# A decoder's linear attention on one Trainium2 core: one reciprocal, keys by a maximum, sums in one pass

## The reference, cut to what matters

```python
for i in range(8):
    residual = x
    Q  = elu(x @ Wq[i] + bq[i]) + 1
    Kf = elu(x @ Wk[i] + bk[i]) + 1
    V  = x @ Wv[i] + bv[i]
    KV, sumK = sum over positions of Kf * V, of Kf
    Z  = 1 / (Q * sumK + 1e-6)
    att = Q * KV * Z
    x = layer_norm(gelu(att @ Wo[i] + bo[i]) + residual)
    residual = x
    x = layer_norm(gelu(gelu(x @ W1[i] + b1[i]) @ W2[i] + b2[i]) + residual)
```

## Time and profile before

| what | value |
|---|---|
| median of three runs | 3417.19 us (3416.45 to 3419.0) |
| span of the profiled execution | 3428.6 us |
| PE, DVE busy | 88%, 79% of the span |
| ACT, POOL busy | 56%, 39% |

### The profile page before, as it was taken

The page is one execution under the profiler, slowest core; times in us unless marked ns, Lnnn a source line. Parts: engine busy times, 40 slices in busy tenths (PEclk is TensorE's granted clock), DMA queues, the critical chain, the costliest instruction groups (busy, mean ns, idle before and its releaser), DMA issues. The chain is left out here.

```text
span 3428.6 us, 44182 instructions
## 1 busy us (share of the span) xinstructions
PE 3029.2 (88%) x11560; PEld 2029.0 (59%) x11561; DVE 2711.6 (79%) x8902; ACT 1927.6 (56%) x2995; POOL 1323.7 (39%) x1039
## 2 busy tenths in 40 slices
PE   5698989898989898999899989998999976998995
PEld 4465656565656565666566655665566644776553
DVE  8879888988898889888988898889888834763111
ACT  4566666666666666666666666666666622442221
POOL 5325343534353435343534353435443323333002
PEclk9899999999999999999999999999999987997998
DMA  4001100100011001000100010001000001003312
GB/s 102 17 1 24 25 16 18 24 25 16 18 24 25 16 18 24 25 16 18 24 25 16 18 24 25 16 18 24 18 24 4 1 0 49 0 0 131 100 40 74
DMA packets 212286, 93.22 MB, mean 27 GB/s; under 512 B 146792, under 2 KB 207984, under 8 KB 212048
## 3 DMA queue, kind: packets, MB, share of 16 engines
q1 hardware_dynamic: 209408, 83.30, 9.6%
q0 software_dynamic: 2640, 7.21, 0.6%
HBM read 80.24 MB, written 10.22 MB: 26 GB/s over the span
## 5 line engine op out<-in xcount | busy, mean ns | idle before, releaser
L350 PE MATMUL PS<-XTHI,WHI 128*128 128x512 f32 x1536 | 672.6, 438 | 38.1 <-DVE EK L654 27.9
L285 POOL TENSOR_TENSOR INV<-INV,CE 128x512 f32<-128x512 f32 x256 | 305.9, 1195 | 984.1 <-DVE INV L697 984.1
L646 DVE SCALAR_TENSOR_TENSOR RK<-RK,EK 128x128 f32<-128x128 f32 x1024 | 599.6, 638 | 28.7 <-ACT RK L515 0.5
L351 PE MATMUL PS<-XTLO,WHI 128*128 128x512 f32 x1536 | 610.7, 398 | 0.0
L352 PE MATMUL PS<-XTHI,WLO 128*128 128x512 f32 x1536 | 609.9, 397 | 0.0
L398 PE MATMUL Y<-ATT,WO 128*128 128x512 f32 x1024 | 468.5, 612 | 59.8 <-POOL ATT L289 59.4
L398 PE MATMUL Y<-H,W2S 128*128 128x512 f32 x1024 | 465.9, 609 | 51.9 <-DVE R L708 50.4
L289 POOL TENSOR_TENSOR ATT<-INV,CC 128x512 f32<-128x512 f32 x256 | 316.7, 1237 | 195.5 <-PE Y L398 177.9
L398 PEld LDWEIGHTS Y<-ATT,WO 128*128 128x128 f32 x1024 | 197.7, 196 | 301.0 <-issue 298.2
L350 PEld LDWEIGHTS PS<-XTHI,WHI 128*128 128x128 f32 x1536 | 291.4, 190 | 133.2 <-issue 42.3
L398 PEld LDWEIGHTS Y<-H,W2S 128*128 128x128 f32 x1024 | 197.0, 195 | 290.4 <-issue 227.2
(11 more groups left out here) (195 smaller groups left out, 5440.7 us busy)
## 6 DMA issues: line engine op xcount, KB each, us to landing
STAGE<-L_attn_Wk SPq DMA_DIRECT2D x128, 64.0 KB, 2.1
STAGE<-L_attn_Wv SPq DMA_DIRECT2D x128, 64.0 KB, 2.1
STAGE<-L_attn_Wq SPq DMA_DIRECT2D x128, 64.0 KB, 2.1
WO<-L_attn_Wo SPq DMA_DIRECT2D x8, 1024.0 KB, 5.5
W2S<-L_attn_W SPq DMA_DIRECT2D x8, 1024.0 KB, 6.1
STAGE<-L_attn_W SPq DMA_DIRECT2D x64, 128.0 KB, 3.7
RAW<-L_ffn_r_gate SPq DMA_DIRECT2D x8, 512.0 KB, 3.5
RAW<-L_ffn_r_up SPq DMA_DIRECT2D x8, 512.0 KB, 3.6
```

The lines of the kernel that those rows point to most:

```text
L285: nc.gpsimd.tensor_tensor(r3, r3, spread(CE[:, e, :], SEQ), ALU.mult).then_inc(att_s, 1)
L350: nc.tensor.matmul(out, whi[:, kc, :], xhi[:, kc, :], start=(kc == 0), stop=False)
L351: nc.tensor.matmul(out, whi[:, kc, :], xlo[:, kc, :], start=False, stop=False)
L646: ins = nc.vector.scalar_tensor_tensor(RK[:, p, seq(b)], RK[:, p, seq(b)], 0.0, EK[:, p, seq(b)], ALU.add, ALU.add, accum_out=SUMK[:, p, b ...
```

## The change

In the attention stack alone:

- ACT no longer computes `RK`, nor log and exp of the denominator. Its table set for the attention is the one with exp alone. A small `BUP` = key bias + 1 is made twice a layer.
- Keys: `KK[.., 0, ..]` = the larger of (PSUM + `BUP`) and the rounded exp, one DVE instruction over 512; `KK[.., 1, ..]` = that times V, one instruction over 512; then one reduction over both (1024 elements to 8 sums, `SUMS`).
- Four operations on 128x4 (`factors`) in place of five; they move from the end of `keys` to the start of `queries`.
- One DVE reciprocal of 128x512, in place in `EQ`, directly behind the denominator, in place of log, exp, `residues` and `inverses`. `attend` reads `EQ`.
- PE waits for `kf` (DVE) where it waited for `rk` (ACT), and for `kv_mul` where it waited for `kv_sum`. ACT waits for `att` where it waited for `recip` before it overwrites `EQ`.

```diff
+        BUP = sb("BUP", [P, HC])
...
-        EK = sb("EK", [P, 2, TOK])
-        RK = sb("RK", [P, 2, TOK])
+        KK = sb("KK", [P, 2, 2, TOK])
...
-        INV = sb("INV", [P, IRING, TOK])
...
-        SUMK = sb("SUMK", [P, 2, TS])
-        KVS = sb("KVS", [P, 2, TS])
-        RSK = sb("RSK", [P, 2, TS])
+        SUMS = sb("SUMS", [P, 2, 2, TS])
...
@@ -280,8 +276,8 @@
                 g, e = l * TILES + t, c % IRING
                 n = g * HC + c
                 pool.wait_ge(recip, n + 1)
-                pool.wait_ge(stat, n * 5 + 5)
-                r3 = INV[:, e, :].rearrange("p (b s) -> p b s", b=TS)
+                pool.wait_ge(stat, n * 4 + 4)
+                r3 = EQ[:, e, :].rearrange("p (b s) -> p b s", b=TS)
                 nc.gpsimd.tensor_tensor(r3, r3, spread(CE[:, e, :], SEQ), ALU.mult).then_inc(att_s, 1)
                 pool.wait_ge(att_s, n + 1)
...
 
-                return [(rk, n - 1), (kv_sum, n - 1), (rq, n - 1)]
+                return [(kf, n - 1), (kv_mul, n - 1), (rq, n - 1)]
...
                     if m < 3:
-                        pe.wait_ge((rk, kv_sum, rq)[m], chunks)
+                        pe.wait_ge((kf, kv_mul, rq)[m], chunks)
...
                 if t == 0 and c % 4 == 0:
                     cs = slice(c, c + 4)
                     act.wait_ge(ba_in[c // 4], (l + 1) * 48)
+                    nc.scalar.add(BUP[:, cs], BA[:, 0, cs], 1.0)
                     nc.scalar.mul(BNEG[:, :, cs], BA[:, :, cs], -1.0).then_inc(b_neg, 1)
                     act.wait_ge(b_neg, 2 * l + (c // 4 + 1))
                 act.wait_ge(k_mm, n + 1)
                 if not (type(n) is int and n < 2):
                     act.wait_ge(kv_sum, n - 1)
-                nc.scalar.activation(EK[:, p, :], PS[:, half, :], ACT.Relu, scale=-1.0,
+                nc.scalar.activation(KK[:, p, 0, :], PS[:, half, :], ACT.Relu, scale=-1.0,
                                      bias=BNEG[:, 0, c:c + 1]).then_inc(nk, 1)
-                nc.scalar.activation(RK[:, p, :], PS[:, half, :], ACT.Relu, bias=BA[:, 0, c:c + 1]).then_inc(rk, 1)
                 act.wait_ge(nk, n + 1)
-                nc.scalar.activation(EK[:, p, :], EK[:, p, :], ACT.Exp, scale=-1.0).then_inc(ek, 1)
+                nc.scalar.activation(KK[:, p, 0, :], KK[:, p, 0, :], ACT.Exp, scale=-1.0).then_inc(ek, 1)
                 act.wait_ge(q_mm, n + 1)
                 if not (type(n) is int and n < IRING):
-                    act.wait_ge(recip, n - (IRING - 1))
+                    act.wait_ge(att, n - (IRING - 1))
                 nc.scalar.activation(EQ[:, c % IRING, :], PS[:, half + 2, :], ACT.Relu, scale=-1.0,
...
 
-            def invert(l, t, c):
-
-                n, e = (l * TILES + t) * HC + c, c % IRING
-                act.wait_ge(denom, n + 1)
-                if not (type(n) is int and n < IRING):
-                    act.wait_ge(att, n - (IRING - 1))
-                nc.scalar.activation(INV[:, e, :], EQ[:, e, :], ACT.Ln).then_inc(log, 1)
-                act.wait_ge(log, n + 1)
-                nc.scalar.activation(INV[:, e, :], INV[:, e, :], ACT.Exp, scale=-1.0).then_inc(inv, 1)
-
             def attention_tables():
 
-                nc.scalar.preload_act_table_set("natural_log_exp_and_others")
+                nc.scalar.preload_act_table_set("exp_and_others")
...
                 if exists(l, t + 2):
-                    invert(nl, nt, 7)
+                    attention_tables()
                     al, at = slot_of(l, t + 2)
                     chunk(al, at, 0)
...
                 n = (l * TILES + t) * HC + c
                 p, e, half = c % 2, c % IRING, 3 * (c % 2)
                 dve.wait_ge(ek, n + 1)
-                nc.vector.tensor_scalar(EK[:, p, :], EK[:, p, :], -1.0, 1.0, ALU.add, ALU.add).then_inc(k_exp, 1)
-                dve.wait_ge(rk, n + 1)
+                nc.vector.tensor_scalar(KK[:, p, 0, :], KK[:, p, 0, :], -1.0, 1.0, ALU.add, ALU.add).then_inc(k_exp, 1)
+                if t == 0 and c % 4 == 0:
+                    dve.wait_ge(b_neg, 2 * l + (c // 4 + 1))
                 dve.wait_ge(k_exp, n + 1)
-                for b in range(TS):
-                    ins = nc.vector.scalar_tensor_tensor(RK[:, p, seq(b)], RK[:, p, seq(b)], 0.0, EK[:, p, seq(b)],
-                                                         ALU.add, ALU.add, accum_out=SUMK[:, p, b:b + 1])
-                ins.then_inc(k_sum, 1)
+                nc.vector.scalar_tensor_tensor(KK[:, p, 0, :], PS[:, half, :], BUP[:, c:c + 1], KK[:, p, 0, :],
+                                               ALU.add, ALU.max).then_inc(kf, 1)
                 dve.wait_ge(v_mm, n + 1)
-                if t == 0 and c % 4 == 0:
-                    dve.wait_ge(ba_in[c // 4], (l + 1) * 48)
-                dve.wait_ge(k_sum, n + 1)
-                for b in range(TS):
-                    ins = nc.vector.scalar_tensor_tensor(EK[:, p, seq(b)], PS[:, half + 1, seq(b)], BA[:, 1, c:c + 1],
-                                                         RK[:, p, seq(b)], ALU.add, ALU.mult,
-                                                         accum_out=KVS[:, p, b:b + 1])
-                ins.then_inc(kv_sum, 1)
-                nc.vector.tensor_scalar(SUMK[:, p, :], SUMK[:, p, :], TINY, None, ALU.max).then_inc(stat, 1)
-                dve.wait_ge(stat, n * 5 + 1)
-                nc.vector.reciprocal(RSK[:, p, :], SUMK[:, p, :]).then_inc(stat, 1)
-                dve.wait_ge(stat, n * 5 + 2)
-                nc.vector.tensor_scalar(ES[:, p, :], RSK[:, p, :], EPS_ATT, None, ALU.mult).then_inc(stat, 1)
+                dve.wait_ge(kf, n + 1)
+                nc.vector.scalar_tensor_tensor(KK[:, p, 1, :], PS[:, half + 1, :], BA[:, 1, c:c + 1], KK[:, p, 0, :],
+                                               ALU.add, ALU.mult).then_inc(kv_mul, 1)
+                dve.wait_ge(kv_mul, n + 1)
+                nc.vector.tensor_reduce(SUMS[:, p, :, :], KK[:, p, :, :].rearrange("p k (b s) -> p k b s", b=TS),
+                                        AX.X, ALU.add).then_inc(kv_sum, 1)
+
+            def factors(l, t, c):
+
+                n = (l * TILES + t) * HC + c
+                p, e = c % 2, c % IRING
                 dve.wait_ge(kv_sum, n + 1)
+                nc.vector.tensor_scalar(SUMS[:, p, 0, :], SUMS[:, p, 0, :], TINY, 1.0 / EPS_ATT, ALU.max,
+                                        ALU.mult).then_inc(stat, 1)
+                dve.wait_ge(stat, n * 4 + 1)
+                nc.vector.reciprocal(ES[:, p, :], SUMS[:, p, 0, :]).then_inc(stat, 1)
+                dve.wait_ge(stat, n * 4 + 2)
                 if not (type(n) is int and n < IRING):
                     dve.wait_ge(att, n - (IRING - 1))
-                nc.vector.tensor_tensor(CC[:, e, :], KVS[:, p, :], RSK[:, p, :], ALU.mult).then_inc(stat, 1)
-                dve.wait_ge(stat, n * 5 + 4)
-                nc.vector.tensor_tensor(CE[:, e, :], CC[:, e, :], ES[:, p, :], ALU.mult).then_inc(stat, 1)
-
-            def queries(l, t, c, before=True):
-
+                nc.vector.scalar_tensor_tensor(CC[:, e, :], SUMS[:, p, 1, :], 1.0 / EPS_ATT, ES[:, p, :], ALU.mult,
+                                               ALU.mult).then_inc(stat, 1)
+                dve.wait_ge(stat, n * 4 + 3)
+                nc.vector.scalar_tensor_tensor(CE[:, e, :], CC[:, e, :], -1.0, ES[:, p, :], ALU.mult,
+                                               ALU.mult).then_inc(stat, 1)
+
+            def queries(l, t, c):
 
                 n = (l * TILES + t) * HC + c
                 p, e = c % 2, c % IRING
+                factors(l, t, c)
                 dve.wait_ge(eq, n + 1)
                 nc.vector.tensor_scalar(EQ[:, e, :], EQ[:, e, :], -1.0, 1.0, ALU.add, ALU.add).then_inc(q_exp, 1)
-                if before and not (type(n) is int and n < 1):
-                    residues(n - 1, (c - 1) % HC)
                 dve.wait_ge(rq, n + 1)
                 dve.wait_ge(q_exp, n + 1)
-                dve.wait_ge(stat, n * 5 + 3)
                 for b in range(TS):
                     ins = nc.vector.scalar_tensor_tensor(EQ[:, e, seq(b)], EQ[:, e, seq(b)], ES[:, p, b:b + 1],
                                                          RQ[:, p, seq(b)], ALU.add, ALU.add)
                 ins.then_inc(denom, 1)
-                if before and not (type(n) is int and n < 1):
-                    inverses(n - 1, (c - 1) % HC)
-
...
+                dve.wait_ge(denom, n + 1)
+                nc.vector.reciprocal(EQ[:, e, :], EQ[:, e, :]).then_inc(recip, 1)
...
-                    queries(nl, nt, 7, False)
+                    queries(nl, nt, 7)
                 if exists(l, t + 2):
                     al, at = slot_of(l, t + 2)
-                    n = (g + 2) * HC
-                    residues(n - 2, HC - 2)
-                    inverses(n - 2, HC - 2)
-                    residues(n - 1, HC - 1)
-                    inverses(n - 1, HC - 1)
```

(38 more changed lines are left out.)

## The result

The changed kernel takes 3817.9 us (median of four runs, 3813.8 to 3820.6) against 3418.1 us before: 11.6% slower, ratio 1.1164 with a 95% interval of 1.1148 to 1.118. The forecast was 3643 us, so the sign was right and the size about half of what came (226 us said, 400 measured).

What follows compares the result with a forecast made beforehand. PE and DVE were taken as near-equal bounds, DVE setting the end after the change. Reciprocal +791, holding -399 and filled waits -166 gave +226 us: span 3655, median 3643 us, 6.6% slower; range 3480 to 3820.

Steps and rivals of the forecast that it cites:

- DVE becomes the bound, one for one: Attention stack: work added to DVE beyond 5.2 us a slot lengthens the slot one for one; PE waits longer.
- The reciprocal's price: DVE's 128x512 reciprocal in each chunk: 5.9 ns an element, 3.17 us, giving +791 us of DVE time.
- the three prices that I weighed: Reciprocal's cost an element above the floor, from small reciprocals: 4.5, 5.9 or 7.25 ns; 5.9, from the longer row, taken.
- The unheld chunk: DVE's chunk with nothing in the way: 6.05 us before, and again 6.05 us after, leaving the whole reciprocal over.
- The waits filled: DVE's waits for exp and inverse fill up: -166 us, as DVE would lag behind ACT and PE instead.
- The holding: DVE held by POOL on the sums (L646) and Newton steps: all of it goes, -399 us.
- holding comes back elsewhere: Rival: POOL holds roundings, small operations and denominators for half of what is saved, +200, 3843 us; chance 0.08.
- the signs that I had named: Right: reciprocal near 3.2 us, exp waits almost gone, more PE waiting. Wrong: reciprocal under 2.3 us, denominators' mean far above 350 ns.
- a steeper reciprocal: Rival: DVE's reciprocal costs 7.25 ns an element, 179 us more, 3822 us; chance 0.17.
- two other rivals: Holding comes back elsewhere (3843 us, chance 0.08); DVE's waits don't fill, up to +166, 3809 us, chance 0.08.

Runs made afterwards that it cites:

- Half the reciprocal: The changed kernel with the reciprocal over the first 256 of its 512 columns, the other half left uninverted: 3464.3 us, ratio 1.0115.
- the passes moved ahead: The changed kernel with GpSimd's two attend passes of chunks 2 and 5 issued ahead of the norms' rstd: 3722.5 us, ratio 1.0857.
- ATT elsewhere: The changed kernel with the two passes to ATT done by ScalarE (four activations a chunk), none by GpSimd: 3621.1 us, ratio 1.0555.
- the keys' part alone: The kernel before with only the change's keys' maximum, product, reduction and four small operations; log, exp and Newton steps stay: 3268.1 us, ratio 0.9541.
- the reciprocal alone: The kernel before with only the reciprocal replacing log, exp, residues and inverses; keys computed as before: 3775.4 us, ratio 1.103.

## Why the prediction was right in its sign and half in its size

- *DVE becomes the bound, one for one.* Right. DVE's waits for inputs were 166 us and are 1.4. Half the reciprocal, the passes moved ahead, and ATT elsewhere each moved the time by what they took from DVE, less the waits that came back: 354 for 410 - 56, 95 for 97, 197 for 206 + 22 - 26. TensorE's lower clock is not what lengthened the kernel: it carries no part of these, and DVE waited for PE only three times, at the end of the stack. I did not try to hold the clock up by itself.
- *The reciprocal's price.* 3.17 us said, 3.35 measured: 47 us too few. Of the three prices that I weighed, the one from the longer row was the nearest.
- *The unheld chunk.* Without the reciprocal 6.05 us said. 9.06 less 3.27 for the reciprocal from start to start is 5.79: 67 us too many, since behind the product, the reduction and the denominators the next one starts 0.03 to 0.04 us after the end (1593.05 + 0.75 to 1593.84, 1593.84 + 1.22 to 1595.09, 1596.42 + 1.14 to 1597.59) and not 0.11. With the reciprocal's 47 us that is 771 where 791 was said. But this is a chunk with nothing else in it. Over all chunks, worked out as for the keys' part, it grew by 2.80 us and not by 3.01, or 717 us.
- *The waits filled.* 166 said, some 178 measured with those put down to issue.
- *The holding.* This is the term that failed: "What follows `attend`'s start is now the rounding, the two PSUM operations and the reduction", and the denominators "start ... 4.8 us behind the reciprocal's end, when POOL's two passes ... are done", from which I took off the whole 399 us. The sums and the Newton steps did lose it, and PSUM operations and reduction were not held once. But I looked at one chunk's distance and not at GpSimd's queue. There the passes of chunks 2 and 5 wait behind `rstd`, which the statistics free just ahead of the denominators. And `attend` was never the only one that holds: in the trace before, by longest overlap, 104 us of the sums' holding lie beside it, 126 beside the second norm's scale and bias (L318, L320) and 116 beside splits of weights, which the Newton step does not start. So denominators, queries' rounding and small operations took up 303 us, while the norm's scaling and the keys' rounding lost 58: 536 became 382, a gain of some 153 and not 399. The rival "holding comes back elsewhere", at 3843 us and a chance of 0.08, was the case that came, by 246 us where it said 200.

The terms as measured are +717, -153 and -178, or +386 us against the 387 by which the spans differ. The clean chunk's 771 would have left 53 us over. The trace puts some 30 of them at chunks 7 and 0, which together grew by 5.09 us and not by 6.02: there the kernel before ran two chunks' Newton steps one behind the other. Some 20 lie at chunks 3 to 6, with a residual or a norm among their operations, which grew by 2.79 to 2.91 us each. That these have fewer dependent starts to pay is argued and not tried.

Of the signs that I had named, a reciprocal near 3.2 us, passes of 0.75 and 1.22 us and waits for exp almost gone came. Others spoke against me: the denominators' mean is 516 ns, far above 350, and PE waits less for `X1LO` and `ATT` (7.3 and 27.9 us, before 101.4 and 59.4), not more. The measured 3818 us lies 2 us inside the range's upper end of 3820, which was drawn for a steeper reciprocal and a part of two other rivals. That it still holds the result is luck.

The Trainium skill's repeat count of 8 (VectorE: DVE Perf Modes, Walkthrough: the 8-slice pipeline in each mode), read as eight cycles, gave an estimate of 4.4 us for the instruction and 3970 us in all. The measured 6.25 ns an element are six cycles at its 0.96 GHz. The measurement decides.

## What to carry to other kernels

- An instruction's price at full size can be had from small ones by the slope above the floor of an ordinary one: 178 and 207 ns at 4 and 8 elements gave 3.17 us at 512, and 3.35 was measured. An operation that is dear per element does not belong on the engine that is one of two near-equal bounds, however many others it replaces.
- Time that an engine is held by a neighbour is not saved in full by moving the work that is held now. Of the 359 us on the sums some 94 came back on other operations with the keys' part alone, and of 399 us some 245 with both parts. List what else is exposed, and read the neighbour's queue for what releases it, and when.
- Take a change of several parts apart before giving it up: here one part was worth -4.6% by itself.

## What the runs showed of the hardware that I had not expected

- DVE's reciprocal costs 153 ns and 6.25 ns an element: 178, 1753 and 3353 ns for 4, 256 and 512 elements, where a rounding of 512 takes 0.42 us and passes over two tensors take 680 to 750 ns.
- It was never held by GpSimd (3352 to 3355 ns; with the reciprocal alone, 71 of 242 had GpSimd at work beside them), nor were the reduction (1219 to 1222) and the operations with one PSUM input (750 to 755), with GpSimd beside 101 and some 140 of 241. A rounding of one SBUF tile, an operation on two, and operations on as few as 4 elements were, for up to 2.2 us beyond their median (the sums before, 2495 against 287 ns; denominators, 1981 against 347; the first small operation 1836 against 170). Taking two of GpSimd's passes away (382 to 176 us of holding), and GpSimd at work beside all 412 held instructions, show that it is GpSimd that holds.
- The Trainium skill (SBUF — State Buffer, Who interferes with whom) divides them so. Outside the modes that use two ports, an operation with at most one SBUF input keeps to DVE's own ports, and a reduction always does. One with two SBUF inputs contends with a GpSimd instruction that reads SBUF, and a `tensor_scalar` can enter a two-port mode and contend too. The runs agree, if the roundings are in such a mode: they take 0.42 us where two tensors of 512 take 0.68. The reciprocal, with one SBUF input, goes with the first.
- Fewer and longer instructions did not make the unheld chunk shorter: with the keys' part alone it is 0.57 us longer in the mean over all chunks. The keys' part won because its long operations, two that read PSUM and a reduction, were never held (265 us less holding in all).
